# A decoder kernel on one Trainium2 core: the two quantised feed-forward stages written out over groups, with another order of their steps

## The chip, the core and the metric

The kernel runs on one core of a Trainium2 chip. The core's engines work side by side, each through its own list of instructions, and wait for each other on semaphores: TensorE (PE: matrix products and transposes into PSUM), VectorE (DVE), ScalarE (ACT), GpSimd (POOL) and SyncE (SP, which issues the DMAs). The metric is the device time of one execution in microseconds (us). Three runs of the kernel before gave 1752.78, 1754.56 and 1755.44 us; the median is 1754.56.

## What is computed

A decoder of four layers on x of 16 sequences x 128 tokens x 128 features. Each layer adds an attention, a cross attention and a feed-forward block, each applied to the layer norm of x. The change touches the feed-forward blocks of layers 0 and 1 alone. Cut to what matters:

```python
# layer 0, on the layer norm of x; a row is one token
def _weight_quant(w):
    scale = 1.0 / jnp.clip(jnp.mean(jnp.abs(w)), 1e-05)
    return jnp.clip(jnp.round(w * scale), -1.0, 1.0) / scale
def _act_quant(x):
    scale = 127.0 / jnp.clip(jnp.max(jnp.abs(x), axis=-1, keepdims=True), 1e-05)
    return jnp.clip(jnp.round(x * scale), -128.0, 127.0) / scale
def _bitlinear(x, w):                   # 128 -> 512 (gate, up), 512 -> 128 (down)
    return jnp.einsum('bsi,oi->bso', _act_quant(x), _weight_quant(w))
# x + down(silu(gate(x)) * up(x))

# layer 1: the same, with a root mean square norm of the rows first
def bitlinear(x, w, b):
    xn = x * jax.lax.rsqrt(jnp.mean(jnp.square(x), axis=-1, keepdims=True) + 1e-06)
    return jnp.einsum('bsi,oi->bso', activation_quant(xn), weight_quant(w)) + b
# x + bitlinear(gelu(bitlinear(x, w1, b1)), w2, b2)
```

## The kernel before

X stays in SBUF for the whole kernel. The stages follow each other in the order L0a, L0x, L0f, L1a, L1x, L1f, L2a, ..., L3t (layer and block: a attention, x cross attention, f feed-forward). The 16 sequences go through each stage in four groups (GROUPS = 4) of four sequences (GB = 4), so a group's rows are a tile of 128 tokens x 4 x 128 features, and its inner rows HID one of 128 x 4 x 512. The order of instructions on each engine is written by hand; signals (`signal(name, {stage: per group})`) are semaphores, `x.at(p, it, k)` is the value that signal x has after item k of group `it`.

The quantised stages L0f and L1f are `bit_ffn` on PE (L1140), ACT (L1738) and DVE (L2347). Before their groups, DVE does `quantise_weights` (L2314): the sums of absolute values of three weights (L2319), the mean over partitions by a product on PE (L1171), the scales, then three rounding steps, of which the second and third run over all three weights at once (L2327, L2329, L2331). It then quantises the first group's input (`quantise_input`, L2334). Three groups run in a loop with a register (`Fori`), the fourth is written out behind it. One group goes as follows:

- PE transposes the rounded input XN of the group (L1143) into PSUM bank 7, ACT copies it to XQT and takes the rounding constant off (L1740), and PE forms the inner rows of the four sequences (L1149, and L1151 for the second product of L0f, into banks 4 to 7; L1f has one product). In L0f PE waits ahead of it for X's update of the group before, since bank 4 holds the down product.
- DVE meanwhile takes the moments of the next group's X (`next_moments`, L1961), POOL forms the root of the variance (`ln_root`, L556), and DVE writes the next group's normed rows into XN (`next_normed`, L1976), once PE has transposed the old ones.
- L0f: ACT applies Silu (L1746), DVE multiplies by the second product (L2358), drains and takes the row's largest magnitude (L2288), sequence by sequence. L1f: DVE adds the bias (L2352), ACT applies Gelu (L1749), and then the four sums of squares (L1753) and those of the next input (L1735); POOL forms the root (`root`, L588).
- DVE forms the quantisation factors of the inner rows (`factors`, L2290: three or four instructions on 128x4 elements, each behind a drain), rounds the inner rows (L2312), then does magnitude, factors and rounding of the next input.
- PE transposes the rounded inner rows (L1163), one sequence at a time, each followed by the down product (L1157) of the sequence before it, into bank 4; ACT copies each transposed piece in between (L1759).
- DVE waits for the down product (`y_psum`) and adds it to X (L2372, or L2374 and L1986).

Rounding is by adding and taking off the constant ROUND. `drain` makes DVE wait until its earlier instructions have written their results. In the cross attentions L0x and L1x, which come just before the quantised stages, DVE's last steps are the softmax inputs (L2079, L2083) and then `normalise` (L2090, L2094) of the last two sequences.

## Time and profile before

| | |
|---|---|
| median of three runs | 1754.56 us (1752.78 to 1755.44) |
| the profiled execution, its own time | 1752.75 us |
| span of its trace | 1751.0 us |
| mean granted TensorE clock over the span | 0.829 of full speed |
| busy: PE, DVE, ACT, POOL | 1248.0, 1150.0, 780.1, 165.1 us |
| share of the chain that ended last: PE, DVE, ACT | 50%, 22%, 9% |

Times are in us from the start of the span. A row of a timeline gives start, duration, engine, line, operation, output <- input, the count of merged instructions, and in brackets how long the engine stood idle before it and what released it. A row of the stretches gives for each engine its busy time and, in brackets, the number of instructions, then PEclk, the granted TensorE clock (1.00 is 2.4 GHz, 0.50 is 1.2 GHz). A row of the groups gives line, engine, operation and shapes, the count, then busy us and mean ns of one, then the idle time before them and what ended it. "issue" is a wait for nothing that the profile shows.

### The profile page before, as it was taken

What the parts mean: (1) busy time and instruction counts of PE and PEld (TensorE: products, weight loads), DVE (VectorE), ACT (ScalarE), POOL (GpSimd) and SP (SyncE); (2) the same over time, 40 slices, a digit from 0 to 9 for tenths busy, and PEclk for the clock granted to TensorE, in tenths of its full rate; (3) what the DMA queues carried; (4) which work ended last, traced back from release to release, by engine and by line L of the source; (5) the groups of instructions that cost most, each with busy time, mean ns of one, the idle gap of its engine ahead of it and who ended that gap; (6) DMA issues with size and microseconds to landing.
All of it is one profiled execution on the core that took longest, in us unless ns stands there. A gap on an engine that the chain in (4) does not pass through costs nothing.

```text
span 1751.0 us, 24843 instructions
## 1 busy us (share of the span) xinstructions
PE 1248.0 (71%) x8870; PEld 822.9 (47%) x8882; DVE 1150.0 (66%) x2830; ACT 780.1 (45%) x1466; POOL 165.1 (9%) x139
## 2 busy tenths in 40 slices
PE   4998889964599999989953488988888940000485
PEld 2655555532468888845532354555554420000353
DVE  2655457877656676568857666777675449998354
ACT  1544346654354454436646432666342413433242
POOL 2210101300000000011101000120000000000121
PEclk7888798986799999979976777899899975555698
DMA  3000300000000000000000000000000330000100
GB/s 118 13 13 11 143 7 7 8 1 0 1 1 1 1 1 1 7 7 13 7 1 0 1 1 7 7 7 1 1 0 1 78 78 0 0 0 14 50 16 19
DMA packets 28857, 28.16 MB, mean 16 GB/s; under 512 B 12240, under 2 KB 23504, under 8 KB 27856
## 3 DMA queue, kind: packets, MB, share of 16 engines
q1 hardware_dynamic: 28752, 26.76, 5.2%
q8 instruction: 66, 1.08, 0.3%
q14 instruction: 39, 0.32, 0.1%
HBM read 20.20 MB, written 6.55 MB: 15 GB/s over the span
## 4 chain that ended last, share of the span: by engine, by line
PE 50%; DVE 22%; issue 13%; ACT 9%; DVEq 2%; POOL 2%; DMA 1%; SPq 1%; POOLq 0%; ACTq 0%
PE PSA L892 3%; PE PSA L1045 3%; PE PSA L882 3%; PE PSA L1330 2%; PE PSA L732 2%; DVE BIG L2637 2%; PE PSA L738 2%; PE PSA L715 2%; PE PSA L1062 2%; PE PSA L1025 2%; PE PSA L999 2%; ACT BIG L1602 2%; PE PSA L1011 2%; PE PSA L1006 2%; DVE BIG L2629 2%
## 5 line engine op out<-in xcount | busy, mean ns | idle before, releaser
L1609 ACT ACTIVATE QK<-PSA 128x512 f32<-128x512 f32 x192 | 104.7, 595 | 110.3 <-PE PSA L892 110.1
L1360 PE MATMUL PSA<-ROWS,ONES 1*128 1x512 f32 x8 | 5.4, 760 | 204.5 <-DVE BIG L2676 204.5
L2083 DVE TENSOR_TENSOR BIG<-PSA,MX 128x1024 f32<-128x1024 f32 x96 | 117.5, 1224 | 12.2 <-PE PSA L892 9.3
L882 PE MATMUL PSA<-BIG 32*128 32x512 f32 x384 | 114.3, 685 | 15.0 <-DVE BIG L2083 13.9
L2079 DVE TENSOR_REDUCE MX<-PSA 128x8 f32<-128x1024 f32 x96 | 116.8, 1217 | 6.3 <-PE PSA L882 5.7
L556 POOL TENSOR_TENSOR RSTD<-VEPS,HALF 128x4 f32<-128x4 f32 x41 | 41.7, 1016 | 817.9 <-DVE VEPS L1964 817.9
L1602 ACT ACTIVATE BIG<-BIG 128x1024 f32<-128x1024 f32 x96 | 101.7, 1059 | 25.2 <-DVE BIG L2083 25.2
L892 PE MATMUL PSA<-K,BIG 128*128 128x128 f32 x768 | 107.0, 285 | 6.4 <-ACT BIG L1602 4.8
L892 PEld LDWEIGHTS PSA<-K,BIG 128*128 128x128 f32 x768 | 90.8, 146 | 40.1 <-ACT BIG L1602 28.1
L562 POOL TENSOR_SCALAR BIG<-BIG,COLS 128x512 f32<-128x512 f32 x52 | 80.5, 1565 | 261.0 <-ACT BIG L1594 140.5
L1360 PEld LDWEIGHTS PSA<-ROWS,ONES 1*128 1x128 f32 x8 | 1.4, 214 | 207.1 <-issue 207.0
L1163 PE MATMUL PSA<-K,BIG 128*128 128x128 f32 x128 | 31.1, 408 | 73.2 <-DVE BIG L2312 73.2
L1901 ACT ACTIVATE BIG<-BIG 128x64 f32<-128x64 f32 x128 | 39.5, 372 | 84.9 <-DVE BIG L2637 84.9
L1045 PE MATMUL PSA<-BIG,QK 128*128 128x65 f32 x512 | 64.9, 270 | 8.1 <-DVE QK L2193 8.0
L1045 PEld LDWEIGHTS PSA<-BIG,QK 128*128 128x128 f32 x512 | 63.1, 192 | 13.0 <-issue 12.7
L1675 ACT ACTIVATE QK<-PSA 128x512 f32<-128x512 f32 x64 | 38.3, 598 | 59.1 <-PE PSA L1035 59.1
L904 PE MATMUL PSA<-QK,VE 128*9 128x128 f32 x1536 | 60.8, 277 | 0.1
L1163 PEld LDWEIGHTS PSA<-K,BIG 128*128 128x128 f32 x128 | 23.9, 219 | 78.0 <-DVE BIG L2312 78.0
L2006 DVE TENSOR_REDUCE MX<-PSA 128x8 f32<-128x1024 f32 x32 | 39.1, 1221 | 29.2 <-PE PSA L738 28.9
L1546 ACT ACTIVATE QK<-PSA 128x512 f32<-128x512 f32 x64 | 34.9, 596 | 49.2 <-PE PSA L748 49.2
L2176 DVE TENSOR_REDUCE MX<-PSA 128x8 f32<-128x1024 f32 x32 | 39.1, 1222 | 20.5 <-PE PSA L1025 20.5
L1976 DVE TENSOR_SCALAR XN<-X,MV,RSTD 128x128 f32<-128x128 f32 (+1 forms) x164 | 47.0, 350 | 6.2 <-POOL RSTD L556 5.6
(390 smaller groups left out, 3053.7 us busy)
## 6 DMA issues: line engine op xcount, KB each, us to landing
CTX<-in_ctx_t SPq DMA_DIRECT2D x16, 256.0 KB, 3.2
W<-in_w SPq DMA_DIRECT2D x1, 2048.0 KB, 7.2
W<-in_w SPq DMA_DIRECT2D x1, 1412.0 KB, 11.7
ROWS<-in_rows SPq DMA_DIRECT2D x1, 1232.0 KB, 8.8
scratch_q<-TMP SPq DMA_DIRECT2D x4, 256.0 KB, 2.0
W<-scratch_q SPq DMA_DIRECT2D x64, 16.0 KB
W<-in_w SPq DMA_DIRECT2D x2, 512.0 KB, 10.6
scratch_q<-BIG SPq DMA_DIRECT2D x4, 256.0 KB, 2.3
```

The source lines that it names most:

```text
L556: pool.tensor_tensor(RSTD[:, 0, :], VEPS[:, 0, :], HALF[:], ALU.pow).then_inc(ln_rstd.sem, 1)
L562: ins = pool.tensor_scalar(KM[:, new % 2, :, r, :], tile(KN[:, new % 2, :]), col("lane", r), None, ALU.mult)
L882: mm = pe.matmul(banks[n], QN[r, it % 2, tok(i)], KM[r, it % 2, i].rearrange("p r t -> p (r t)"), start=p != "L1x", stop=True, skip_group_ ...
L892: mm = pe.transpose(PS[4 + c][:, tok(j)], PH[:, m % 2, tok(4 * c + j)], ident)
L904: mm = pe.matmul(PS[6][STRIP * j:STRIP * j + HD + 1, tok(2 * h + c)], VE2[:, it % 2, n % GB, 8 * h + 4 * c + j, :], PT[:, m % 2, c, tok(j) ...
L1045: mm = pe.matmul(dst[:, x * 65:(x + 1) * 65], PT[:, m % 2, r, tok(x)], V1[:, pair % 2, s, 8 * h + 2 * x + r, :], start=True, stop=True)
L1163: mm = pe.transpose(PS[i][:, tok(c)], HID[:, i, tok(c)], ident)
L1602: act.activation(PH[:, m % 2, :], PH[:, m % 2, :], ACT.Exp, scale=float(HD) ** -0.5).then_inc(exp_ready.sem, 1)
L1609: act.activation(PT[:, m % 2, c, :], PS[4 + c], ACT.Copy).then_inc(p_ready.sem, 1)
L1976: ins = dve.tensor_scalar(XN[:, i, :], seq(next_group(it), i), MV[:, i, 0:1], RSTD[:, 0, i:i + 1], ALU.subtract, ALU.mult)
L2079: dve.tensor_reduce(high, s, AX_X, ALU.max).then_inc(max_taken.sem, 1)
L2083: dve.tensor_tensor(tile(PH[:, m % 2, :], 8), s, last(high, P), ALU.subtract).then_inc(shifted.sem, 1)
```

## The change

Both stages are written out over all four groups, on PE, ACT, DVE and POOL. The steps of DVE stand in another order: X's update comes at the end of a group behind the next normed rows and the moments of the group after that; the factors of inner rows and of the next input are formed together on 128x8 elements; in L1f the two roots are one on POOL, also on 128x8. The weight sums are taken in the cross attention before, and the weights are rounded one by one (L1f rounds w1 once instead of twice). In L0f a semaphore (`multiplied`) stands in the place of the drain between multiply and magnitude. PE transposes all four inner tiles first, then does two down products, the next input's transposes, and the other two; the down product goes to bank 6, so that only the third and fourth sequence of L0f's second product wait for X's update. In L1f ACT takes each sum of squares right behind the next Gelu. The diff, cut to its core:

```diff
--- before.py
+++ after.py
@@ POOL @@
                 if p == "L1f":
-                    root(p, 0, 0)
-                    with pool.Fori(0, GROUPS - 1) as it:
-                        ln_root(p, it)
-                        root(p, it, 1)
-                        root(p, it + 1, 0)
-                    ...
+                    ln_root(p, 0)
+                    for n in range(GROUPS + 1):
+                        pool.wait_ge(rms_stats, n + 1)
+                        pool.tensor_tensor(RR[:], VR[:], mid(HALF[:], 2), ALU.pow).then_inc(rms_root, 1)
+                        if n + 1 < GROUPS:
+                            ln_root(p, n + 1)
+                    continue
@@ PE @@
+                def up(g):
+                    pe.wait_ge(xqt_ready.sem, xqt_ready.at(p, g))
+                    for i in range(GB):
+                        mm = pe.matmul(PS[i], XQT[:, tok(i)], WQ[:, 0, :], start=True, stop=True)
+                        if p == "L0f":
+                            if i == 2 and g:
+                                pe.wait_ge(x_updated.sem, x_updated.at(p, g - 1))
+                            mm = pe.matmul(PS[4 + i], XQT[:, tok(i)], WQ[:, 1, :], start=True, stop=True)
+                        mm.then_inc(h_psum.sem, 1)
...
+                for g in range(GROUPS):
+                    for i in range(GB):
+                        pe.wait_ge(hq_ready.sem, hq_ready.at(p, g, i))
+                        for c in range(4):
+                            mm = pe.transpose(PS[i][:, tok(c)], HID[:, i, tok(c)], ident)
+                        mm.then_inc(hqt_psum.sem, 1)
+                    down(g, 0)
+                    down(g, 1)
+                    if g + 1 < GROUPS:
+                        input_t(g + 1)
+                    down(g, 2)
+                    down(g, 3).then_inc(y_psum.sem, 1)
+                    if g + 1 < GROUPS:
+                        up(g + 1)
@@ ACT, L1f @@
                         for i in range(GB):
                             act.wait_ge(pre_ready.sem, pre_ready.at(p, g, i))
                             act.activation(HID[:, i, :], HID[:, i, :], ACT.Gelu).then_inc(act_ready.sem, 1)
+                            if i:
+                                hidden_squares(g, i - 1)
+                        hidden_squares(g, GB - 1).then_inc(h_squares.sem, 1)
@@ DVE, cross_attention, behind the last softmax inputs @@
+                following = run[run.index(p) + 1:][:1]
+                if following and following[0] in BIT:
+                    weight_sums(following[0])
                 normalise(GROUPS * GB - 2)
                 normalise(GROUPS * GB - 1)
@@ DVE @@
+            def quantise_weight(p, m):
+                n = BIT_WEIGHTS[p][m]
+                dve.tensor_scalar(WTMP[:, m, :], w(f"{p}.{n}"), WSC[:, 2, m:m + 1], ROUND, ALU.mult, ALU.add)
+                dve.drain()
+                dve.tensor_scalar(WTMP[:, m, :], WTMP[:, m, :], ROUND, 1.0, ALU.subtract, ALU.min)
+                dve.drain()
+                dve.tensor_scalar(WQ[:, m, :], WTMP[:, m, :], -1.0, None, ALU.max).then_inc(wq_ready, 1)
...
+                dve.drain()
+                input_magnitude()
+                if p == "L1f":
+                    dve.memset(VR[:, 1, :], 1.0)
+                    dve.wait_ge(x_squares.sem, x_squares.at(p, 0))
+                    mean_square(0, P).then_inc(rms_stats, 1)
+                next_moments(p, 0)
+                weight_scales(p)
+                quantise_weight(p, BIT_PARTS[p][0])
+                if p == "L1f":
+                    dve.wait_ge(rms_root, 1)
+                dve.drain()
+                factors(0, 1)
+                quantise_input()
+                input_scales()
+                for m in BIT_PARTS[p][1:]:
+                    quantise_weight(p, m)
+                next_normed(p, 0)
+                next_moments(p, 1)
+
+                for g in range(GROUPS):
+                    more = g + 1 < GROUPS
                     if p == "L0f":
+                        for i in range(GB):
+                            dve.wait_ge(act_ready.sem, act_ready.at(p, g, i))
+                            dve.scalar_tensor_tensor(HID[:, i, :], PS[4 + i], DQ[:, 1, i:i + 1], HID[:, i, :], ALU.mult, ALU.mult
+                                                     ).then_inc(multiplied.sem, 1)
+                            if i:
+                                magnitude(i - 1)
+                        if more:
+                            input_magnitude()
+                        magnitude(GB - 1)
                     else:
+                        for i in range(GB):
+                            dve.wait_ge(h_psum.sem, h_psum.at(p, g, i))
+                            dve.scalar_tensor_tensor(HID[:, i, :], PS[i], DQ[:, 0, i:i + 1], row("L1f.b1"),
+                                                     ALU.mult, ALU.add).then_inc(pre_ready.sem, 1)
+                        if more:
+                            input_magnitude()
+                        for i in range(GB):
+                            magnitude(i)
+                        if more:
+                            dve.wait_ge(x_squares.sem, x_squares.at(p, g + 1))
+                            mean_square(0, P)
+                        dve.wait_ge(h_squares.sem, h_squares.at(p, g))
+                        mean_square(1, INNER).then_inc(rms_stats, 1)
+                        dve.wait_ge(rms_root, g + 2)
+                    dve.drain()
+                    factors(0 if more else 1, 2)
+                    for i in range(GB):
+                        dve.tensor_scalar(HID[:, i, :], HID[:, i, :], QS[:, 1, i:i + 1], ROUND, ALU.mult, ALU.add).then_inc(hq_ready.sem, 1)
+                    if more:
+                        quantise_input()
+                        input_scales()
+                    dve.tensor_scalar(DQ[:, 2, :], AM[:, 1, :], WSC[:, 1, 2:3], 1.0 / 127.0, ALU.mult, ALU.mult)
+                    if more:
+                        next_normed(p, g + 1)
+                    dve.drain()
+                    if g + 2 < GROUPS:
+                        next_moments(p, g + 2)
+                    update(g)
```

## Rows read from the trace of the kernel before

**Rows 1.** The page: busy time of each engine.

```profile
PE 1248.0 (71%) x8870; PEld 822.9 (47%) x8882; DVE 1150.0 (66%) x2830; ACT 780.1 (45%) x1466; POOL 165.1 (9%) x139
```

**Rows 2.** Stretches of L0f and L1f: length, then busy time by engine.

```profile
405.12:459.70 54.58, 22.27 (x129) 16.12 (x132) 41.45 (x130) 22.68 (x31) 3.02 (x3) 0.75 0.00 0
459.70:466.54 6.84, 4.75 (x32) 3.81 (x32) 3.03 (x9) 2.73 (x4) 0.00 (x0) 0.73 0.00 0
903.66:925.77 22.11, 3.16 (x9) 1.65 (x10) 16.47 (x49) 8.21 (x22) 4.82 (x4) 0.50 0.00 0
925.77:982.80 57.03, 20.22 (x117) 15.63 (x120) 44.17 (x145) 33.01 (x71) 9.06 (x9) 0.68 0.00 0
```

**Rows 3.** Timeline: VectorE at the end of L0x and the start of L0f.

```profile
380.14 0.26 DVE L2090 RECIPROCAL RD<-PSA 128x16 f32<-128x16 f32 x1 [4.32 <-PE PSA L913]
...
385.16 1.87 DVE L2319 TENSOR_REDUCE WSC<-W 128x1 f32<-128x512 f32 x3
...
388.27 1.28 DVE L2327 TENSOR_SCALAR BIG<-W,WSC 128x512 f32<-128x512 f32 x3
...
390.66 0.96 DVE L2331 TENSOR_SCALAR BIG<-BIG 128x1536 bf16<-128x1536 f32 x1
```

**Rows 4.** Timeline: the second group of L0f.

```profile
412.68 0.87 DVE L1952 BATCH_NORM_STATS2 ST<-X 128x6 f32 x4 [0.62 <-issue]
...
414.33 1.01 POOL L556 TENSOR_TENSOR RSTD<-VEPS,HALF 128x4 f32<-128x4 f32 x1 [16.90 <-DVE VEPS L1964]
415.37 1.11 DVE L1976 TENSOR_SCALAR XN<-X,MV,RSTD 128x128 f32 x4 [1.12 <-POOL RSTD L556]
416.40 0.74 DVE L2358 SCALAR_TENSOR_TENSOR BIG<-PSA,DQ,BIG 128x512 f32<-128x512 f32 x1
417.22 0.69 DVE L2288 TENSOR_REDUCE AM<-BIG 128x1 f32<-128x512 f32 x1
...
423.02 1.67 DVE L2312 TENSOR_SCALAR BIG<-BIG,QS 128x512 f32<-128x512 f32 x4
...
429.62 1.13 DVE L2372 SCALAR_TENSOR_TENSOR X<-PSA,DQ,X 128x128 f32 x4 [1.75 <-PE PSA L1157]
```

**Rows 5.** Timeline: TensorE in L0f, low clock and high clock.

```profile
394.24 1.12 PE L1143 MATMUL PSA<-K,XN 128*128 128x128 f32 x4 [6.50 <-DVE XN L2312]
...
408.99 0.61 PE L1163 MATMUL PSA<-K,BIG 128*128 128x128 f32 x4
...
410.88 0.65 PE L1143 MATMUL PSA<-K,XN 128*128 128x128 f32 x4
...
423.57 1.97 PE L1163 MATMUL PSA<-K,BIG 128*128 128x128 f32 x8 [9.21 <-DVE BIG L2312]
...
425.46 0.61 PE L1157 MATMUL PSA<-BIG 128*128 128x128 bf16 x4
```

**Rows 6.** Stretches of L0f: the granted clock beside TensorE's busy time.

```profile
405.12:408.60 3.48, 2.94 (x15) 2.62 (x16) 3.03 (x9) 1.37 (x2) 0.00 (x0) 0.50 0.00 0
...
419.10:428.80 9.70, 5.06 (x28) 4.35 (x28) 7.68 (x23) 2.62 (x4) 0.00 (x0) 0.50 0.00 0
...
451.30:456.40 5.10, 0.00 (x0) 0.00 (x0) 4.22 (x9) 1.21 (x3) 0.70 (x1) 1.00 0.01 2
```

**Rows 7.** Timeline: first bias instruction of L1f's first and second group.

```profile
917.21 2.73 DVE L2352 SCALAR_TENSOR_TENSOR BIG<-PSA,DQ,ROWS 128x512 f32<-128x512 f32 x4 [0.48 <-remote]
...
936.34 2.73 DVE L2352 SCALAR_TENSOR_TENSOR BIG<-PSA,DQ,ROWS 128x512 f32<-128x512 f32 x4
```

**Rows 8.** Groups of instructions by line: roots on POOL.

```profile
L588 POOL TENSOR_TENSOR RSTD<-VEPS,HALF 128x4 f32<-128x4 f32 x12 | 12.1, 1006 | 129.0 <-DVE VEPS L2209 89.6 <-DVE VEPS L2387 39.5
...
L593 POOL TENSOR_TENSOR RD<-RD,HALF 128x2 f32<-128x2 f32 x1 | 0.7, 697 | 208.8 <-DVE RD L2650 208.8
```

**Rows 9.** Timeline: ScalarE in L1f's last group.

```profile
975.12 2.60 ACT L1749 ACTIVATE BIG<-BIG 128x512 f32<-128x512 f32 x4 [3.56 <-DVE BIG L2352]
...
977.75 0.63 ACT L1753 ACTIVATE QK<-BIG 128x512 f32<-128x512 f32 x1
```

More of the change, by code:

```diff
@@ L49 @@
 BIT = ("L0f", "L1f")
+BIT_PARTS = {"L0f": (0, 1, 2), "L1f": (0, 2)}
+BIT_WEIGHTS = {"L0f": ("gate", "up", "down"), "L1f": ("w1", "w1", "w2")}
 BEFORE_LOOP = -1
@@ L1167, in bit_ffn @@
-                down(GB - 1).then_inc(y_psum.sem, 1)
+                input_t(0)
+                quantised_weights = sum(len(BIT_PARTS[q]) for q in quantised[:quantised.index(p) + 1])
+                pe.wait_ge(wq_ready, quantised_weights - 1)
+                up(0)
+                pe.wait_ge(wq_ready, quantised_weights)
+                for g in range(GROUPS):
[12 more added lines that the diff above has]
+                        up(g + 1)
@@ L1478, in _ @@
                     pe.wait_ge(taps_ready, 1)
-                if p in ("L0f", "L1f"):
+                if p in BIT:
                     weight_means(quantised.index(p) + 1)
-                    pe.wait_ge(wq_ready, quantised.index(p) + 1)
+                    pe.wait_ge(x_updated.sem, x_updated.before[p])
+                    bit_ffn(p)
+                    continue
                 if p == "L1a":
@@ L2763, in _ @@
                     continue
-                if p in ("L0f", "L1f"):
-                    quantise_weights(p, quantised.index(p) + 1)
+                if p in BIT and (n == 0 or run[n - 1] not in CROSS3):
+                    weight_sums(p)
                 if p == "L3t":
```

246 lines of the change are left out of this document (103 added, 143 removed).

## The prediction, made before the changed kernel ran

> **What bounds the kernel now.** I read the page first, then the stretches of the two quantised stages, then their instructions in order of time. TensorE is busy for 71% of the span and VectorE for 66% [rows 1], but such a share is an average over twelve stages, and the change touches only two: L0f, from 385.1 to 466.54, and L1f, from 903.66 to about 991, 169 us of a span of 1751.0 us. In the three full periods of L0f VectorE is busy for 41.45 of 54.58 us, TensorE for 22.27, ScalarE for 22.68; in L1f 44.17 of 57.03 us against 20.22 and 33.01 [rows 2]. So these stages go by VectorE's program order, and what counts is its work and the places where it stands still.
>
> I call T the moment at which VectorE begins to round the inner rows of a group. The first T of L0f is at 405.12 and the fourth at 459.70, three periods of 18.2 us; in L1f they are at 925.77 and 982.80, three of 19.0 [rows 2].
>
> One L0f group in order of time [rows 4]: after X's update 0.62 us pass at the loop's edge, moments take from 412.68 to 414.33, the root on POOL to 415.34, the next normed rows to 416.40, four pairs of multiply and magnitude to 422.2, factors to 423.02, rounding 1.67 us. Then come the input's magnitude, a second chain of factors, its rounding, and a wait for the down product, until X is updated at 429.62. All of it is one chain.
>
> **The change, part by part, L0f.** A VectorE instruction without a drain starts about 0.09 us before the last one ends (four roundings of 0.48 take 1.67); with a drain it starts 0.08 after.
>
> Start of the stage. X is complete just before 385.16 and T is 405.12 [rows 2, 3]. The weight sums (1.87 us) and the wait for their mean go into the cross attention, where VectorE stands still for 4.32 us before 380.14 [rows 3]; cost there nothing, and if that gap were gone it would be 1.87 us. Rounding weight by weight costs more than before: three instructions of 0.48 us with drains, 1.58 us each, 4.7 for three, where 3.35 us stood (388.27 to 391.62 [rows 3]; that a third of the 0.96 us instruction takes 0.48 is my estimate from the 128x512 row beside it, bounds 0.32 and 0.48). The second group's moments move ahead too. In sum from 385.14: magnitude 0.60, moments 1.48, scales 0.48, gate 1.66, factors 0.75, input rounding 0.80, scales 0.26, up and down 2.99, normed rows 1.18, moments 1.48: the first multiply at 396.8. From there 6.55 us to T (below): T = 403.4, a gain of 1.7 us.
>
> A period of L0f, from T = 0. Inner rounding to 1.58, input rounding to 2.38, scales to 2.9. Then VectorE wants to form the next normed rows, which overwrites what TensorE must first transpose, and that is queued on TensorE behind four transposes of the inner rows and two down products. **This is the new wait**, and behind it on VectorE stand the moments, the X update and every multiply. Its end: transposes start at 0.54; each group's four take 0.91 us at the low clock (eight matmuls 1.97 us from first start to last end), 0.5 at the high one; down products 0.42 or half of it; the input's transposes 1.1 or 0.65 [rows 5]. All low: 0.54 + 3.64 + 0.84 + 1.1 = 6.1. In the trace the clock rose between 3.5 and 3.9 us after T in the first group, and not before 5.8 us after T in the second [rows 5, 6]; with a rise at 3.6 the same sum is 5.0. I take 5.8, since the rise comes mostly in the midst of this burst. Then normed rows 1.11, drain, moments 1.48, X update 1.13, drain: 3.9 us, and TensorE's next products and the first Silu are done by then (the transposed input reaches the products by 7.2, the first Silu ends at 9.0; the last two pairs wait for X, 1.6 us after its update, and VectorE asks for them 2.0 after). Then multiply and magnitude interleaved: 4 multiplies at 0.66, 3 magnitudes and the input's at 0.60, the last 0.69 and a drain, 5.8; one chain of factors 0.75. In all 5.8 + 3.9 + 5.8 + 0.75 = **16.2 us**, where 18.2 stood (the last of three 15.6, it has no input). Removed are the loop's edge 0.62, the root's wait 1.06, four drains 0.6, a chain of factors with its drains 0.85 and the wait for the down product (1.75 in this group), added is the wait of 2.9. Sum: 54.6 - 48.1 = 6.5 us. The tail after the last T (6.84 us [rows 2]) stays as it is: all transposes come before the down products, but the last product waits for the same ScalarE copy. **L0f: 1.7 + 6.5 = 8.2 us.**
>
> **L1f.** Here a POOL root stands in every group's path, now on 128x8 elements instead of 128x4. Not in the trace; its roots take 697 ns on two columns and 1006 on four [rows 8], so 154 ns a column and 1.62 us for eight. Bounds: 1.0 (no growth) and 2.0 (doubled). From the first bias instruction to T before: 8.56 us (917.21 to 925.77 [rows 2, 7]). After: ScalarE starts 0.79 later and runs four Gelu and four Square, 5.27 us, whatever their order; mean square 0.25, root 1.66, factors 0.98: 8.9 us. The next normed rows (1.1) leave this part, but ScalarE was its bound, so that gives nothing. From T to the next first bias before: 10.57 us (925.77 to 936.34 [rows 7]). After: 5.8, normed rows and moments 2.66, bias and X update 1.98: 10.4. Period **19.4 against 19.0**, a loss of 1.1 us over three. The second factor chain and the second root wait, some 3 us, are removed, but the wait for the transposes takes their place. The start: X complete at 903.66 [rows 2]. POOL first clears its buffer (1.8 us, as before), then the layer norm's root, then the wide one: input factors can start at 908.9, first bias at 914.9; a table load (1.28) before Gelu puts Gelu at 916.0, T at 924.2 against 925.77: a gain of 1.6. Tail: 0.3. **L1f: 0.8 us.**
>
> No DMA is moved; SP's queue is untouched. POOL's roots in L0f are hidden, their results are asked for a group later. Table loads: each loop turn held two of 1.28 us; the body that is already written out has none. I cost them at nothing: ScalarE had time for them.
>
> **Sum.** 8.2 + 0.8 = 9.0 us. The profiled execution took 1752.75 us (span 1751.0 and 1.75 around it), so 1743.7 by its own time. The median of the three runs is 1754.56, 1.8 above it, so I forecast **1745.5 us**.
>
> **Rivals.** (a) Small gain: the clock stays low through every burst (wait ends at 6.1, 0.35 us in six periods, 2 us) and the wide root doubles (0.4 us five times, 2 us): gain 5 us, 1749.5. For it: [rows 2] show clocks of 0.68 to 0.75 over the periods, so much of each is low. Against it: the rise came before the end of this burst in most groups. With a further miss in the start it falls within no change.
>
> (b) The clock stays up between bursts in L0f. TensorE's idle time between its last product and the next transposes shrinks from 9.2 us [rows 5] to 5 to 6; the granted clock was still 1.00 over 5.10 us of idleness (451.30 to 456.40) before it fell [rows 6]. If bursts start high, the wait ends at 3.7 instead of 5.8: 2.1 us in three periods, 6 us more, 1739.5. Against it: in other groups it fell sooner, and L1f's pauses stay at 10 us and more. The Trainium skill (TensorE: Matmul & The Clock Gate, HAM oscillation) says that pauses between bursts let the clock fall and that each burst then starts at half rate; by that, closing the pauses is worth the same 6 us, and the trace agrees as far as each burst here starts at 1.2 GHz.
>
> (c) Slower: ScalarE in L1f now alternates Gelu and Square. If the two were in different tables, each change would load one at 1.28 us: five in the chain from the first Gelu to the last Square, four groups, 25.6 us, net 16.6 us slower, 1762. One load within each group is already enough to halve the gain, and two to undo it (10 us). Against it: in the last group of L1f Squares follow Gelus at 977.75, at once and with no load [rows 9], so both are in one table. The Trainium skill (ScalarE: Activation LUTs, Rules for kernel authors) says to finish one table set before the next; it speaks against this order only if the sets differ, and the row says that they don't.
>
> (d) The change doesn't do what it says: the sums don't fit into the cross attention's gap or the written-out code is issued late; gain 2 us, 1752.5.
>
> **How the numbers follow.** Forecast (gain 6.5 to 12) 0.60; (a) 0.17; (b) 0.12; (c) 0.04; (d) 0.07. A measurement of this kernel can tell about 0.2%, 3.5 us, from no change. Forecast and (b), and most of (a), lie beyond it: faster 0.86; (d) and a share of (a): same 0.10; slower 0.04. The range takes in the bounds of the wait (5.0 to 6.1: gains 14 to 7), of the root (gain 3 more to 2 less), and (a) and (b): 1739 to 1751.
>
> **What would show it.** Right: periods of T near 16.2 in L0f and 19.4 in L1f; VectorE waiting 2 to 3.5 us for TensorE before each next-normed instruction; root on 128x8 near 1.6 us; no table load within the groups; first T 1.7 and 1.6 us sooner after X. Wrong: table loads between Gelu and Square, a first Silu that VectorE waits for, or a period of L0f above 17.

## The result, and the profile after

The changed kernel takes 1729.35 us (median of four runs, 1728.97 to 1733.73) against 1754.52 of the kernel before, a ratio of 0.9863, 95% interval 0.9846 to 0.9881. That is 25.2 us faster, where I had forecast 9.0 and a range that ended at 1739. Its profiled execution took 1733.73 us, with a span of 1731.9; the one of before took 1752.75.

The page of the kernel after, busy time by engine, beside [rows 1]:

```profile
PE 1244.7 (72%) x8873; PEld 825.3 (48%) x8882; DVE 1141.1 (66%) x2811; ACT 766.5 (44%) x1456; POOL 165.6 (10%) x136
```

Over the whole kernel each engine's busy time is within 14 us of what it was (VectorE 8.9 us less), so the gain has to be looked for stage by stage. The stretches of the two quantised stages, after (length; busy time of PE, PEld, DVE, ACT, POOL; granted clock; DMA), beside [rows 2]:

```profile
390.07:408.19 18.12, 4.28 (x11) 1.76 (x12) 16.25 (x55) 4.39 (x6) 2.02 (x2) 0.50 0.00 0
408.19:454.50 46.31, 22.14 (x130) 17.34 (x132) 36.04 (x110) 17.79 (x27) 2.02 (x2) 0.72 0.00 1
454.50:460.79 6.29, 4.42 (x32) 4.07 (x32) 2.94 (x9) 2.64 (x4) 0.00 (x0) 0.73 0.00 0
894.80:915.18 20.38, 2.57 (x7) 1.14 (x8) 15.73 (x59) 7.88 (x22) 7.24 (x5) 0.50 0.00 0
915.18:969.49 54.31, 18.08 (x119) 15.46 (x120) 38.68 (x118) 26.88 (x67) 6.92 (x5) 0.69 0.00 1
969.49:976.71 7.22, 4.63 (x32) 4.28 (x32) 3.63 (x10) 2.75 (x4) 0.00 (x0) 0.73 0.00 0
```

The three periods of L0f take 46.3 us instead of 54.6, those of L1f 54.3 instead of 57.0. Less work on VectorE is a large part of that, and not pauses alone: in L0f's periods it is busy for 36.04 us instead of 41.45, 5.4 of the 8.3 us gained; in L1f's for 38.68 instead of 44.17, so there its work fell by 5.5 us and its pauses grew by 2.8. The periods one by one are 16.3, 16.5 and 13.5 us in L0f and 18.3, 19.3 and 16.7 in L1f: the third is shorter than the others in both stages. VectorE in the first group of L0f, after, in order of time, beside [rows 4]:

```profile
408.19 1.68 DVE L2456 TENSOR_SCALAR BIG<-BIG,QS 128x512 f32<-128x512 f32 x4
...
414.06 1.12 DVE L2013 TENSOR_SCALAR XN<-X,MV,RSTD 128x128 f32<-128x128 f32 x4 [3.01 <-PE PSA L1155]
415.26 0.87 DVE L1987 BATCH_NORM_STATS2 ST<-X 128x6 f32<-128x128 f32 x4
...
416.74 1.12 DVE L2396 SCALAR_TENSOR_TENSOR X<-PSA,DQ,X 128x128 f32<-128x128 f32 x4
417.95 1.41 DVE L2431 SCALAR_TENSOR_TENSOR BIG<-PSA,DQ,BIG 128x512 f32<-128x512 f32 x2
...
424.49 1.67 DVE L2456 TENSOR_SCALAR BIG<-BIG,QS 128x512 f32<-128x512 f32 x4
```

One wait stands in the group, 3.01 us for the input's transposes (L1155), ahead of the next normed rows. Moments, X update and first multiplies follow without a pause. In the third group no moments stand between normed rows and update:

```profile
446.16 1.11 DVE L2013 TENSOR_SCALAR XN<-X,MV,RSTD 128x128 f32<-128x128 f32 x4 [2.33 <-PE PSA L1155]
447.37 1.12 DVE L2396 SCALAR_TENSOR_TENSOR X<-PSA,DQ,X 128x128 f32<-128x128 f32 x4
```

Now all stages. This table is my own, from the traces: us from the last X update of one stage to the last of the next; "tail" is L3a with the scan, "end" the rest. Each row is one profiled execution.

```
                    L0a    L0x   L0f    L1a    L1x   L1f   L2a    L2x    L2f   tail    end
before           252.44 132.63 81.47 293.07 144.06 87.51 95.30 140.58 104.97 301.88 114.34
after            257.54 132.53 70.72 289.89 144.13 81.90 90.54 140.03 103.07 301.55 117.24
e1_again         252.32 132.62 70.83 289.87 144.10 81.99 90.57 140.01 103.09 301.91 116.91
e2_l0f_only      257.56 132.52 70.68 289.90 144.14 87.42 94.58 136.30 103.04 301.58 114.32
e3_l1f_only      257.04 132.53 81.28 293.15 144.11 81.70 95.11 138.34 103.06 302.07 117.14
e4_written_out   251.98 132.64 81.41 293.44 144.02 85.04 91.51 138.34 103.76 302.57 118.03
e5_update_early  257.57 132.53 73.14 291.56 143.92 86.27 91.74 136.59 103.06 301.41 114.29
e6_factors_apart 252.69 132.70 72.71 294.32 144.18 82.33 90.52 140.08 103.08 301.84 119.59
e7_pe_order_old  257.68 132.55 76.03 291.24 144.13 86.19 93.16 140.07 103.06 302.15 116.75
e8_input_t_early 257.30 132.53 68.68 291.48 144.15 80.51 92.35 140.03 103.06 301.80 117.05
e9_before_wait3  253.05 132.68 84.56 292.76 144.08 86.43 92.73 136.28 103.04 301.77 114.25
e10_before_wait15 254.90 132.63 82.95 292.07 143.95 87.35 94.51 140.19 103.04 301.68 117.14
e11_after_wait18 257.69 132.51 72.53 292.09 143.96 84.03 92.59 138.31 103.07 301.89 117.13
e12_early_split  251.99 132.65 67.16 290.87 143.90 76.89 95.30 139.87 103.05 301.72 117.11
e13_third_moments 257.96 132.52 72.78 290.84 144.08 84.38 96.39 138.30 103.33 302.37 116.92
e14_before_filler 255.04 132.63 81.42 289.77 144.08 87.43 91.66 140.71 104.99 301.81 114.26
e15_wait_filler  252.38 132.61 72.60 292.17 143.94 84.01 92.59 138.31 103.02 302.28 119.92
e16_early_split_filler 252.01 132.65 68.74 289.00 144.01 76.98 91.65 140.07 103.06 301.59 117.13
```

From before to after L0f gives 10.75 us and L1f 5.61, together 16.4. The rest lies in stages whose code is unchanged: L1a 3.18, L2a 4.76, L2f 1.90, L2x 0.55 and the tail 0.33 us shorter, L0a 5.10 and the end 2.90 longer, net 2.7 in this pair. L0a stands ahead of the change, and the repeated run of the same program has it at 252.32: with that the untouched stages give about 8 us, and 16.4 + 8 is close to the 25.2 us between the medians. The kernel before has one trace only, and its runs in the experiments spread from 1748.6 to 1757.9 us; so what is said below of its untouched stages rests on one execution.

The clock records of these 18 traces can be added up by stage. Here is the length of a stage and, behind the colon, how many us of it TensorE's granted clock was at its lower level, 1.2 GHz:

```
L0a   252.0 to 253.1: 89.5 to 92.9   254.9, 255.0: 96.4           257.0 to 258.0: 110.2, 110.3
L1a   289.0 to 289.9: 13.7           290.8 to 291.6: 17.1 (e8 20.5)
      292.1, 292.2: 19.2 to 20.5     292.8 to 294.3: 23.9 to 24.5
L2x   136.3 to 136.6: 10.2           138.3: 13.7
      139.9 to 140.2: 15.1 to 15.7   140.6, 140.7: 17.7, 17.8
end   114.2 to 114.3: 35.7, 35.8     116.8 to 117.2: 41.7 to 42.1
      118.0: 43.0                    119.6, 119.9: 44.5, 44.8
```

In these four stages the recurring lengths go with the time at the lower level. L2x in the kernel before, in the changed one and in e9:

```profile
1086.47:1227.06 140.59, 120.81 (x1073) 71.88 (x1071) 103.74 (x175) 84.83 (x130) 22.68 (x16) 0.94 0.02 7
```

```profile
1067.25:1207.28 140.03, 120.50 (x1073) 71.60 (x1071) 103.67 (x174) 84.95 (x130) 22.71 (x16) 0.95 0.03 7
```

```profile
1086.30:1222.58 136.28, 116.69 (x1071) 70.12 (x1069) 103.61 (x174) 84.12 (x130) 22.68 (x16) 0.96 0.02 7
```

L2a follows it only loosely (90.5 us with 42.7 at the lower level, 94.6 with 44.4, 95.3 with 49.7, 96.4 with 47.8), L2f not at all (103.05 with 3.4 to 10.2). This is a match of rows; of these stages only L1a has an experiment that sets the level (e14).

### The profile page after: what moved, and what is told of

Read it like the earlier page. It is cut to its first block, busy times and chain, and to the rows that moved or that the text cites. A ratio compares the mean times of both kernels' runs of the same rounds, so it can differ in the third digit from the quotient of the medians.

```text
span 1731.9 us, 24494 instructions
## 1 busy us (share of the span) xinstructions
PE 1244.7 (72%) x8873; PEld 825.3 (48%) x8882; DVE 1141.1 (66%) x2811; ACT 766.5 (44%) x1456; POOL 165.6 (10%) x136
## 4 chain that ended last, share of the span: by engine, by line
PE 52%; DVE 26%; ACT 10%; issue 6%; DVEq 2%; DMA 1%; POOL 1%; SPq 1%; ACTq 0%; POOLq 0%
PE PSA L902 3%; PE PSA L892 3%; PE PSA L1055 3%; PE PSA L1355 2%; PE PSA L742 2%; DVE BIG L2713 2%; PE PSA L748 2%; ACT BIG L1628 2%; PE PSA L725 2%; ACT QK L1635 2%; PE PSA L1072 2%; PE PSA L1035 2%; PE PSA L1009 2%; PE PSA L1021 2%; PE PSA L1016 2%
## 5 line engine op out<-in xcount | busy, mean ns | idle before, releaser
L1055 PEld LDWEIGHTS PSA<-BIG,QK 128*128 128x128 f32 x512 | 63.9, 194 | 13.5 <-issue 13.2
L1183 PEld LDWEIGHTS PSA<-K,BIG 128*128 128x128 f32 x128 | 25.6, 221 | 74.7 <-DVE BIG L2456 56.1
L1572 ACT ACTIVATE QK<-PSA 128x512 f32<-128x512 f32 x64 | 35.2, 596 | 54.3 <-PE PSA L758 54.1
```

The source lines that it names most:

```text
L1055: mm = pe.matmul(dst[:, x * 65:(x + 1) * 65], PT[:, m % 2, r, tok(x)], V1[:, pair % 2, s, 8 * h + 2 * x + r, :], start=True, stop=True)
L1183: mm = pe.transpose(PS[i][:, tok(c)], HID[:, i, tok(c)], ident)
```

## The experiments

Ratios stand against runs of the kernel before on the same chip (their medians were between 1754.18 and 1754.52). In no experiment is part of the computation left out.

**The changed kernel once more.** No edit.

> The changed kernel once more, to get a second trace of it. Theory S (stages): in the first trace L0f lasts 70.7 us from the end of X's update in L0x to its own last update (81.5 before) and L1f 81.9 (87.5 before), 16.4 us less together; both repeat within 2 us. Theory P (pattern): what else differed between the two traces (L0a 5.1 us longer, L1a 3.2, L2a 4.75 and the first group of L2f 1.9 us shorter) is where the stretches of low TensorE clock happened to fall in that one execution, and it comes out otherwise here, by some us in at least one of these stages. Rival R: it repeats in every stage but L0a within 1 us, and belongs to the change. Time in all near 1729 us.

1731.2 us (1728.73 to 1733.9), 0.9885 [0.9855, 0.9915]. Eight of the eleven columns of the table repeat within 0.11 us, the tail and the end within 0.4; L0a doesn't, 252.32 against 257.54, which is the 5 us between 1733.7 and 1728.7. So the 16.4 us are of the change, and in these two traces the times of the untouched stages belong to the program and not to chance, except for L0a.

**One stage at a time.** e2: L0f as changed, L1f with the functions, loop and signals of before. e3 the other way round.

> L0f as changed, L1f as before (its loop, its order, its rounding of weights). Theory S: L0f near 70.7 us, L1f near 87.5. In all 10.8 us less than before (about 1743.7), if nothing outside moves; Rival R (the stage behind a changed one gets faster, because TensorE comes out of it with another clock): L1a also 3 us shorter and L2a as before, about 1740.5. If L2a is 4 to 5 us shorter here too, though nothing just ahead of it was changed, the gain there doesn't belong to L1f's change.

> L0f as before, L1f as changed. Theory S: L1f near 81.9 us, L0f near 81.5; 5.6 us less, about 1749. Rival R: L2a also 4.75 us shorter, about 1744, and L1a as before.

e2: 1734.1 us, 0.9892 [0.986, 0.9923]; L0f 70.68, L1f 87.42. e3: 1746.76 us, 0.997 [0.9956, 0.9983]; L0f 81.28, L1f 81.70. The stages' own gains are independent of each other. L1a goes with L0f (289.9 with it, 293.2 without). L2a goes with neither alone: 94.58 and 95.11, but 90.54 with both.

**Written out, in the old order.** Both stages as in before, with the loop written out on every engine.

```diff
-with dve.Fori(0, GROUPS - 1) as it:
+for it in range(GROUPS - 1):
```

> Both stages in their old order, old signals and old rounding, but the three looped groups written out on all engines. It takes away the pause at the loop's edge on VectorE (0.5 to 0.6 us for each of six periods) and two table loads of 1.28 us in each looped group. My working put the loads at nothing, since ScalarE had time: then the gain is 6 x 0.6 = 3 to 4 us, and the order of steps carries the other 12 to 13 of 16.4. Rival: the loads were on the way (transposed input, first Silu or Gelu): then 2 us more for each looped group or 8 us and more in all, and the new order is worth only half.

1748.59 us, 0.9973 [0.9957, 0.9988]. L0f takes 81.41 us, as before; L1f gains 2.5. VectorE's waits in L0f's groups (us in total, times, longest), before and then written out:

```profile
DVE X L2372 <- PE PSA L1157: 4.2, 3, 1.8
DVE XN L1976 <- POOL RSTD L556: 3.4, 3, 1.1
DVE ST L1952 <- issue: 1.4, 3, 0.6
```

```profile
DVE X L2495 <- PE PSA L1223: 4.1, 3, 1.6
DVE XN L2096 <- POOL RSTD L567: 3.4, 3, 1.1
```

The waits for the down product and for POOL's root stay; only the pause at the edge of a turn (issue) is gone. L0f's sum hides two differences. Its three periods take 53.31 us instead of 54.58, 1.3 less; but its start, up to the first T, takes 21.25 instead of 20.06, 1.2 more. ScalarE loads no table between the groups of e4, and the one load that is left, ahead of the first Silu, stands behind the first product (in the kernel before it began at 396.10, right behind ScalarE's copy), so that VectorE waits for Silu:

```profile
396.88 1.28 ACT L1819 ACT_TABLE_LOAD   x1 [1.17 <-PE PSA L1217]
398.89 0.75 DVE L2481 SCALAR_TENSOR_TENSOR BIG<-PSA,DQ,BIG 128x512 f32<-128x512 f32 x1 [0.97 <-ACT BIG L1819]
```

Another pause, of 0.48 us and without a named releaser, stands ahead of the first factors. So loop edge and loads together were worth 1.3 us in L0f's periods and 1.8 in L1f's (55.2 us instead of 57.0). L0f's 10.75 us are not of writing out alone: they need the rest of the change.

**X updated early again.**

```diff
+                    dve.drain()
+                    update(g)
                     if more:
                         next_normed(p, g + 1)
                     ...
-                    update(g)
```

> The changed kernel with X's update put back ahead of the next normed rows (VectorE waits for the down product first, then for the transposes). In the changed kernel the first multiply of the second and third L0f group starts 9.8 us after T and that of the fourth 7.6. Theory W (the wait for TensorE covers one of the two waits, the update late fills it): here the down product ends at 6.5 to 7.0 us after T, the update at 8.1, normed rows at 9.2, moments at 10.7, so 1 us more in each of six periods, L0f near 73.8 and L1f near 85 us, 5 to 6 us slower in all than the changed kernel. Rival V (the late update is worth nothing, the gain is in what was removed): both stages within 1 us of 70.8 and 81.9.

1735.91 us, 0.9894 [0.9878, 0.9911]. L0f 73.14, L1f 86.27: as these runs have it, the late update is worth 2.4 and 4.4 us. VectorE in e5, first group of L0f:

```profile
408.21 1.68 DVE L2456 TENSOR_SCALAR BIG<-BIG,QS 128x512 f32<-128x512 f32 x4
...
414.44 1.13 DVE L2396 SCALAR_TENSOR_TENSOR X<-PSA,DQ,X 128x128 f32<-128x128 f32 x4 [3.37 <-PE PSA L1171]
415.73 1.12 DVE L2013 TENSOR_SCALAR XN<-X,MV,RSTD 128x128 f32<-128x128 f32 x4 [0.16 <-issue]
```

The wait, 3.01 us for the transposes, becomes 3.37 for the down products, and the next normed rows start 7.5 us after T instead of 5.9.

**Factors apart.** Inner factors ahead of the inner rounding, those of the input behind it.

```diff
-                    factors(0 if more else 1, 2)
+                    factors(1, 2)
                     ...
                     if more:
+                        factors(0, 1)
                         quantise_input()
```

> The changed kernel with two chains of factors again: 128x4 for the inner rows ahead of T, 128x4 for the next input behind the inner rounding. My prediction counted 0.85 us a group as removed. Theory W: VectorE waits 2.2 to 3.3 us for the transposes right behind, and the rounded input is asked for by TensorE only 4.7 us after T, so the second chain disappears in that wait: L0f and L1f within 0.5 us of 70.8 and 81.9. Rival: 0.8 us in each of six periods, 5 us slower.

1738.22 us, 0.9917 [0.9901, 0.9934]. The first two periods of L0f are 16.36 and 16.79 (16.30 and 16.47 with one chain), the third 14.38 instead of 13.54; L1f 0.4 longer.

```profile
403.47 1.67 DVE L2456 TENSOR_SCALAR BIG<-BIG,QS 128x512 f32<-128x512 f32 x4
...
409.42 1.12 DVE L2013 TENSOR_SCALAR XN<-X,MV,RSTD 128x128 f32<-128x128 f32 x4 [2.34 <-PE PSA L1155]
```

The second chain takes its 0.7 us out of the wait for TensorE (2.34 instead of 3.01), and the next step starts at 5.95 us after T as before (5.87). But L0f as a whole takes 72.71 us, 2.0 more, where I had expected at most 0.5: 0.8 in the third period and 0.8 in the tail, in both of which the clock stayed at 0.50 for over 5 us after T, instead of rising between 3 and 4 us after it. The X update of the tail comes 5.96 us after T instead of 5.16:

```profile
456.97 1.13 DVE L2396 SCALAR_TENSOR_TENSOR X<-PSA,DQ,X 128x128 f32<-128x128 f32 x4 [4.15 <-PE PSA L1171]
```

So in the periods in which the clock rises alike, joint factors are worth 0 to 0.3 us; whether the other 1.6 us are of the chain or of where the clock happened to rise, this run doesn't tell.

**TensorE's old order.** Down products between the transposes again, the input's transposes last.

```diff
                         mm.then_inc(hqt_psum.sem, 1)
+                        if i:
+                            down(g, i - 1)
-                    down(g, 0)
-                    down(g, 1)
+                    down(g, 3).then_inc(y_psum.sem, 1)
                     if g + 1 < GROUPS:
                         input_t(g + 1)
-                    down(g, 2)
-                    down(g, 3).then_inc(y_psum.sem, 1)
```

> The changed kernel with TensorE's old order: each down product between the inner transposes, the next input's transposes last. Theory W: these then end 6.4 to 7.1 us after T as in the kernel before, instead of 5.2 to 6.0, and everything on VectorE behind the next normed rows moves by as much: 0.5 to 1.2 us in six periods, 3 to 6 us slower; the wait of VectorE before the next normed rows grows from 2.2-3.3 to 3.5-4.2 us. Rival (VectorE's wait is for something else, or the clock decides alone): within 1 us of the changed kernel.

1745.06 us, 0.9944 [0.9925, 0.9962]; L0f 76.03, L1f 86.19.

```profile
408.35 1.68 DVE L2455 TENSOR_SCALAR BIG<-BIG,QS 128x512 f32<-128x512 f32 x4
...
415.32 1.12 DVE L2012 TENSOR_SCALAR XN<-X,MV,RSTD 128x128 f32<-128x128 f32 x4 [4.12 <-PE PSA L1155]
```

The wait grows by 1.1 us in the first group. TensorE's order is the largest part that was taken back by itself: 5.3 and 4.3 us, where I had expected 3 to 6 in all. 7.9 us of it lie in the periods and 1.7 in the tails, which have no next input. The parts overlap: this one and the late update make 16.4 us, as much as both stages gained, and the starts' 3.7 us are in neither.

**Input transposed earlier still,** behind three of the four inner tiles.

```diff
                         mm.then_inc(hqt_psum.sem, 1)
+                        if i == 2 and g + 1 < GROUPS:
+                            input_t(g + 1)
                     ...
-                    if g + 1 < GROUPS:
-                        input_t(g + 1)
```

> The changed kernel with the next input's transposes between the third and the fourth tile of inner rows. Theory W: they end 4.4 us after T instead of 5.2 to 6.0, VectorE's wait falls to 1.5 us; in the first two periods of each stage 1.3 us less, in the third the update then waits for the down product and it gains nothing: 4 to 5 us faster than the changed kernel over both stages, L0f near 68.5, L1f near 79.5. Rival: the down product comes so much later that the update waits for it in every group; no gain or up to 2 us slower.

1729.98 us (1722.67 to 1733.44), 0.9849 [0.9825, 0.9873].

```profile
407.95 1.67 DVE L2456 TENSOR_SCALAR BIG<-BIG,QS 128x512 f32<-128x512 f32 x4
...
412.34 1.12 DVE L2013 TENSOR_SCALAR XN<-X,MV,RSTD 128x128 f32<-128x128 f32 x4 [1.53 <-PE PSA L1155]
...
415.03 1.12 DVE L2396 SCALAR_TENSOR_TENSOR X<-PSA,DQ,X 128x128 f32<-128x128 f32 x4
```

The wait halves, the update finds its product ready in the first two groups of each stage (in the third it waits 0.9 and 1.3 us, as expected), and the stages take 68.68 and 80.51, 3.4 us less together. But L1a takes 1.6 and L2a 1.8 us more, and nothing of it is left.

**Useless work ahead of the untouched stages.** e9 and e10: the kernel before with four or two extra reductions, with drains, ahead of L0f's last X update (3.1 and 1.5 us). e11: the changed kernel with three, without drains (1.8 us).

```diff
+                if p == "L0f" and not more:
+                    for k in range(4):
+                        dve.tensor_reduce(AM[:, 0, k:k + 1], HID[:, k, :], AX_X, ALU.max)
+                        dve.drain()
```

> The kernel before with four useless reductions (0.77 us each with their drains, 3.1 in all) ahead of the very last X update of L0f, so that L1a starts 3.1 us later against the points at which the TensorE clock can change; nothing else differs. Theory C (L1a's length, 293.1 to 293.4 us where L0f was old and 289.9 where it was new, hangs on where the changes of the clock fall in it, and that on the moment it starts): this start falls where the changed kernel's falls, so L1a takes 289.9 us, and the kernel with 3.1 us more work isn't slower than the kernel before. Rival R (the shorter L1a is a product of the new L0f code, of TensorE's state or of what runs ahead): L1a stays at 293.1 and all comes 3.1 us later.

> The same with two reductions, 1.5 us. Theory C: the start falls near those of the runs with the factors apart and with TensorE's old order, whose L1a took 294.3 and 291.2 us; either, but not 293.1. Rival R: 293.1.

> The changed kernel with three such reductions without drains, 1.8 us, ahead of the last X update of L0f. Theory C: L1a 1.3 to 4.4 us longer than 289.9, so that 1.8 us of work cost 3 to 6 us at the end of L1a. Rival R: 289.9, and 1.8 us in all.

e9: 1750.79 us, 0.9978 [0.9965, 0.9992]. L0f is 3.1 us longer, and the kernel 3.4 us faster: L2a 2.6, L2x 4.3, L2f 1.9 and L1f 1.1 us shorter. e10: 1750.29 us, 0.998 [0.9967, 0.9993]. e11: 1737.47 us, 0.99 [0.987, 0.9929]: between the profiled executions 1.8 us of work cost 6.7, of which L1a 2.2, L1f 2.1 and L2a 2.1, while L2x gave back 1.7. For L1a the expectation of e9 (289.9) was wrong, that of e10 (294.3 or 291.2) too, and that of e11 (1.3 to 4.4 us longer) right: 292.8, 292.1, 292.1. L1f's 2.1 us in e11 come with its code unchanged: in its first and third period the clock stayed at 0.50 for 6 us after T, where it rose between 3 and 4 us after T in the changed kernel, and VectorE's wait ended 6.1 and 6.0 us after T instead of 5.0 and 4.9.

**Both best edits.** e8, and L1f's two roots separate: the input's as soon as its squares are there, the inner rows' by itself.

```diff
-                        pool.tensor_tensor(RR[:], VR[:], mid(HALF[:], 2), ALU.pow).then_inc(rms_root, 1)
+                        pool.tensor_tensor(RR[:, k, :], VR[:, k, :], HALF[:], ALU.pow).then_inc(rms_root, 1)
...
+                            mean_square(0, P).then_inc(rms_stats, 1)
                             input_magnitude()
```

> A version meant to beat both: the next input's transposes between the third and fourth tile of inner rows, and in L1f the root split again into two of 128x4, that of the input started right behind the bias steps, under ScalarE's Gelus and Squares, that of the inner rows alone on the path. The factors stay together. Theory: a root of 1.0 instead of 1.64 us on the path of four groups and 0.8 at the start of L1f: L1f 3 us less than with the transposes alone (80.5), near 77.5; L0f as there, 68.7. In all 3 us less than that version or 3 to 5 less than the changed kernel, near 1726, if the stages that aren't touched don't take it back; they may move by up to 4 us each way with the moment they start. Rival: POOL is held up by its own order (a layer-norm root between the two), and L1f stays at 80 us or above.

1725.97 us (1725.01 to 1726.24), 0.9844 [0.9826, 0.9862]; L0f 67.16, L1f 76.89. POOL's roots in L1f (busy us and mean ns of one), after and then e12:

```profile
L640 POOL TENSOR_TENSOR RR<-VR,HALF 128x8 f32<-128x8 f32 x5 | 8.4, 1672 | 33.5 <-DVE VR L2379 33.5
```

```profile
L644 POOL TENSOR_TENSOR RR<-VR,HALF 128x4 f32<-128x4 f32 x8 | 8.2, 1029 | 30.4 <-DVE VR L2384 30.4
```

POOL works as long in sum, but only 1.03 us of it stand in a group's path instead of 1.64 (1.67 is the mean with the first, which took 1.82), and the input's root comes ahead.

**Moments put back into the third period.**

```diff
                     if g + 2 < GROUPS:
                         next_moments(p, g + 2)
+                    elif more:
+                        moments(lambda i: seq(GROUPS - 1, i), MV)
```

> The changed kernel, with one more set of moments (4 batch statistics, 4 aggregations, two drains, 1.4 to 1.5 us on VectorE, their result used by nothing) behind the last next-normed rows of each quantised stage, where the first two groups have theirs. It tests the step of the prediction that costed the third period. Theory M (my third period was too long because it had moments in it that the code forms ahead): the third period of L0f goes from 13.5 to 14.9 to 15.0 us and that of L1f from 16.7 to 18.1; L0f takes 72.1 (70.72 without), L1f 83.3 (81.9). Rival N (the multiplies wait for Silu or Gelu by then, so the moments would have cost nothing there): the periods stay at 13.5 to 13.9 and 16.7 to 17.0, L0f at 70.7 to 71.1.

1741.78 us (two runs), 0.9928 [0.99, 0.9957]. The third and fourth T of L0f:

```profile
441.36 1.68 DVE L2456 TENSOR_SCALAR BIG<-BIG,QS 128x512 f32<-128x512 f32 x4
...
456.32 1.67 DVE L2456 TENSOR_SCALAR BIG<-BIG,QS 128x512 f32<-128x512 f32 x4
```

A period of 14.96 us, and 18.08 in L1f (956.63 to 974.71): 1.42 and 1.41 more than without, as theory M has it. In L1f the third period also takes 18.13 in e11 and e15, without these moments; but there VectorE's wait ended 6.0 us after T, in e13 4.9 as in the changed kernel, so in e13 the 1.4 us are the moments'. The stages lose 2.1 and 2.5 us; the rest of it lies outside this period, mostly in L0f's tail (6.9 instead of 6.3 us) and in the other parts of L1f.

**Eight useless transposes on TensorE between L0f and L1a,** in the kernel before.

```diff
                 with pe.Fori(0, GROUPS) as it:
                     bodies[p](p, it)
+                if p == "L0f":
+                    for k in range(8):
+                        pe.transpose(PS[0][:, tok(k % 4)], XNT[:, tok(k % 4)], ident)
```

> The kernel before, with 8 more transposes on TensorE (about 1.1 us at the high level, their result used by nothing) between the last down product of L0f and the first transposes of L1a, where TensorE stands idle for 1.54 us. Nothing else moves: L0f stays at 81.5. Theory K (what L1a gains in the changed kernel is the granted clock at its entry: 1.00 over its first 12 us against 0.72 before): the clock stays at 1.00 from 464 on, L1a takes 289.9 to 290.5 instead of 293.07, the total falls by about 3 us if the stages behind it keep their times. Rival S (L1a's time comes from when the stage starts, whatever TensorE did just before): the first 12 us show 0.7 again and L1a 292 to 293.5. Of the stages behind it theory K says nothing; where they change by steps of 2 to 5 us, the granted clock will show it in rows of TensorE.

1746.94 us (1745.6 to 1748.33, six runs), 0.9957 [0.994, 0.9973]. The first 12 us of L1a and the whole of it: before, after, e14.

```profile
466.54:478.54 12.00, 10.85 (x35) 8.02 (x36) 4.05 (x15) 3.55 (x9) 1.22 (x2) 0.72 0.01 2
466.54:759.61 293.07, 275.15 (x2034) 230.59 (x2034) 177.04 (x393) 137.77 (x240) 8.27 (x9) 0.96 0.01 3
```

```profile
460.79:472.79 12.00, 10.85 (x68) 7.88 (x68) 5.81 (x18) 6.08 (x17) 1.22 (x2) 1.00 0.01 2
460.79:750.68 289.89, 271.45 (x2034) 227.45 (x2034) 177.01 (x393) 137.73 (x240) 8.28 (x9) 0.98 0.01 3
```

```profile
469.08:481.08 12.00, 10.84 (x68) 7.88 (x68) 5.80 (x19) 6.07 (x17) 1.22 (x2) 1.00 0.01 3
469.08:758.85 289.77, 271.02 (x2034) 227.01 (x2034) 177.07 (x394) 137.84 (x240) 8.27 (x9) 0.98 0.01 3
```

TensorE is busy 10.85 of those 12 us each time, but counts 68 matmuls at a granted clock of 1.00 and 35 at 0.72 (32 of the 68 are small ones, 64x128, of the next step, which is not yet reached at 0.72). In the kernel before the level fell just after L1a had begun, at the end of an idle time of 1.54 us, and came back some 7 us later. With eight transposes in that gap, of which 0.57 us of idleness was left, it didn't fall, L1a took 3.3 us less, and this with nothing of the change in it. The idle time alone isn't the rule, though: the changed kernel has the same 1.54 us there, unfilled, and kept the level. The other 3.6 us came from L2a (91.66 instead of 95.30), though L1f took the same 87.4.

**The same behind the wait of e11, and in the fastest kernel.** e15: 20 transposes in e11. e16: 8 behind each quantised stage of e12.

> The changed kernel with the 1.8 us of useless reductions ahead of the last X update of L0f (as in e11_after_wait18, where L1a took 292.1 instead of 289.9 and its first stretch ran at the low level) and 20 more transposes on TensorE behind the last down product, so that it works through the 3.3 us in which it stood idle there. L0f 72.5 as in e11. Theory K (level at the entry): high level over L1a's first 12 us, L1a 289.9 to 290.5. Rival S (the shift itself): L1a 292.1 as in e11, with or without the transposes.

> e12_early_split (L0f 67.2, L1f 76.9, 1725.97 us) with 8 more transposes on TensorE behind the last down product of both quantised stages. Theory K: L1a from 290.9 to 289.9 or 290.2; L2a, which starts at the low level in all kernels so far (95.3 in e12), gains 2 to 3 us if the transposes keep the clock up over its first products, as its first 5 to 6 us of TensorE's work run at half rate; total 1722 to 1724. Rival S: L1a 290.9, L2a 95.3 and the total 1726, the transposes change nothing.

e15: 1739.2 us, 0.9916 [0.9891, 0.9941], L1a 292.17: not what theory K gives, for the level was high at L1a's entry but fell within the next 3 us; over the first 12 it was 0.86. e16: 1721.77 us (1721.17 to 1722.43), 0.9815 [0.9795, 0.9836], the fastest of all. L1a 289.00 (290.87 in e12); L2a 91.65 instead of 95.30, with its first 12 us at 0.98 instead of 0.86. L0f took 68.74 where the same code took 67.16 in e12, since the clock rose later in its last two groups; so 1.6 us of a stage's time can lie in that alone. The start of L2a:

```profile
963.39:975.39 12.00, 7.30 (x34) 4.26 (x38) 7.37 (x24) 6.55 (x11) 1.01 (x1) 0.98 0.01 1
```

## Why the prediction was wrong in size

I had 9.0 us and 25.2 were measured. The step that failed by most is the sum over two stages only: it put the others at nothing, with no reason but that the change doesn't touch them, and they gave some 8 us. The second is the third period, which I charged with moments that the code doesn't form there (2.8 us in both stages). Even with both stages sized right, 16.4 us, the sum would have given 1738.1 us, just below my range.

- **Direction and place: right.** Both stages gain, and the new wait for TensorE stands where I put it.
- **Starts: right.** 1.94 and 1.73 us gained, forecast 1.7 and 1.6.
- **First two periods of L0f: right,** 16.3 and 16.5 for 16.2. The wait ended 5.9 and 6.0 us after T (5.8 forecast).
- **Third period: a step that failed.** I gave it 15.6 and 19.4 us, with moments (1.5 us) in it. The code forms moments only while g + 2 is under the number of groups, since two groups' are formed at the stage's start, which I had charged there as well. Measured 13.5 and 16.7; e13 puts them back and has 14.96 and 18.08. That is 1.4 of the 2.1 us missed in L0f and 1.4 of the 2.7 in L1f. Most of the rest is the wait, which ended at 5.2 and 4.9 us after T instead of 5.8.
- **L1f otherwise.** First period 18.3 against 19.4 (wait ended at 5.0), second 19.3. Tail 1.2 us shorter where I had a gain of 0.3. The root on 128x8 took 1.64 us in the groups and 1.82 at the start, for 1.62. In all L1f gave 5.6 where I had 0.8: forecast terms of -1.1, 1.6 and 0.3 came as 2.7, 1.7 and 1.2.
- **L0f in all:** 10.75 for 8.2: start 1.9 (1.7), periods 8.3 (6.5), tail 0.5 (0).
- **Untouched stages: not in my sum at all, some 8 us, the largest miss.** I summed two stages and let the other ten stand. e14 shows for L1a that 3.3 us hang on the clock at its start, which something as small as 1.1 us of TensorE's work decides. The Trainium skill (TensorE: Matmul & The Clock Gate, HAM oscillation) tells of bursts that start at half rate behind pauses as a cost inside a loop; here it is carried over from one stage to the next. For L2a, L2x, L2f and the end no run isolates a cause; L2x and the end go with their time at the lower level in all traces. L2a took 90.5 with its first 12 us at 0.72 and 95.3 at 0.86, so its entry alone doesn't decide it.
- **Rivals.** (a) didn't come: the root was no dearer than computed. (b) didn't either: bursts still began at 0.50 and the periods' mean clock is 0.72, beside 0.75 in [rows 2]; the measured total lay past (b) for other reasons. (c) is out, and its price was wrong: 25.6 us of loads would have made 1745.5 + 25.6 = 1771 us; my 1762 took the gain of 9 off twice. ScalarE's Gelu and Square follow each other at once in L1f's second group, as in [rows 9].

```profile
926.80 0.61 ACT L1771 ACTIVATE QK<-BIG 128x512 f32<-128x512 f32 x1
927.41 0.61 ACT L1788 ACTIVATE BIG<-BIG 128x512 f32<-128x512 f32 x1
```

- **(d)** is out: with the sums in them L0x and L1x took 132.53 and 144.13 us (132.63 and 144.06 before), and the stages gain by themselves (e2, e3). The loop's edge I had at 0.62 us a period in L0f and the table loads at nothing. Writing out gave 1.3 us in L0f's periods, less than the 1.9 of the edges alone, so no cost of the loads shows there; in L1f it gave 2.5 us, of which my sum names none, and e4 doesn't tell edge from loads.

What stays open: what decides when the clock falls, and with it the lengths of L2x (136.3, 138.3, 140.0), L0a (252.3 or 257.6 with one program) and the end; what sets L2a (90.5, 91.7, 92.6, 94.5, 95.3) and L2f. L1a takes 290.9 in e12 with its first 12 us at 1.00, but it has 17.1 us at the lower level further on and at 289.9 only 13.7. No run takes back the weight sums, the rounding weight by weight or the semaphore in place of the drain by themselves, so the starts' 3.7 us are not divided among them.

## What to carry to other kernels

Walk through a written-out loop group by group, with the conditions of each call: what is formed ahead at the start is missing at the end, and a mean period hides it. Order TensorE's queue by who waits: the transposes that free VectorE's next buffer ahead of products that are asked for later gave more here (up to 9.6 us, with the inner transposes drawn together) than any other part that was taken back. And before crediting an edit with its full difference, compare the untouched stages: here a third of the gain came from them, and it can be had, or lost, with work that does nothing.

## What the runs showed of the hardware that I had not expected

- Useless work made the kernel faster: 3.1 us of reductions by 3.4 us (e9; 1.4 to 6.1 by the interval), 1.1 us of transposes by 7.5 us (e14; 4.7 to 10.5). In the changed kernel 1.8 us of it cost 6.7 us (e11).
- Times of untouched stages take recurring values: most agree within 0.1 us in two traces of one program, and jump by 2 to 5 us between programs (L2f mostly 103.05 or 104.98, L2x mostly 136.3, 138.3 or 140.0). In L0a, L1a, L2x and the end they go with the time at 1.2 GHz.
- POOL's root grows by 0.16 us a column: 0.70 us for 128x2 and 1.01 for 128x4 in [rows 8], 1.64 for 128x8 in the groups of L1f.
